# Layers 2 and 3 of a cross-attention chain: scores with the keys on the partitions, two tiles of queries at a time

## The reference

```python
qh = (q_in @ wq + bq).reshape(b, q_len, H, K)        # H = 16, K = 128
kh = (kv_in @ wk + bk).reshape(b, t, H, K)
vh = (kv_in @ wv + bv).reshape(b, t, H, K)
kh = jnp.concatenate([kh, broadcast(bias_k)], axis=1)  # one extra key and value
vh = jnp.concatenate([vh, broadcast(bias_v)], axis=1)
logits = jnp.einsum('bqhk,bthk->bhqt', qh, kh) / sqrt(K)
weights = jax.nn.softmax(logits, axis=-1)
ctx = jnp.einsum('bhqt,bthk->bqhk', weights, vh)
return ctx @ wo + bo
```

## Time and profile before

| | us |
|---|---|
| median of 3 runs | 1865.41 |
| profiled execution, its own time | 1866.31 |
| its span | 1864.4 |
| PE busy | 1711.7 |
| DVE busy | 1217.4 |
| ACT busy | 1018.2 |
| POOL busy | 393.0 |

### The profile page before, as it was taken

One profiled execution on the slowest core, in us unless ns is written; L12 is line 12 of the kernel. 1 busy time (PEld: TensorE's weight loads), 2 busy tenths in 40 slices (PEclk: granted clock), 3 DMA queues, 4 the chain that ended last, 5 costly groups with the idle time before them and its releaser, 6 DMA issues.

```text
span 1864.4 us, 31831 instructions
## 1 busy us (share of the span) xinstructions
PE 1711.7 (92%) x9942; PEld 1462.2 (78%) x9942; DVE 1217.4 (65%) x2487; ACT 1018.2 (55%) x1863; POOL 393.0 (21%) x320
## 2 busy tenths in 40 slices
PE   3698889897789999999999999799999999999997
PEld 2577777786568888888888877688888888888886
DVE  5577777777475666666665766766567566566664
ACT  2466666677344554554554556445455455555563
POOL 4456555542150000000000008410000000000063
PEclk8899999999789999999999999899999999999998
DMA  7767667766032101101101102420111011010021
GB/s 235 193 152 173 173 165 170 174 150 142 18 108 67 67 33 33 66 33 33 66 33 33 66 20 86 100 93 34 33 66 36 30 66 50 16 66 1 1 82 44
DMA packets 114097, 149.53 MB, mean 80 GB/s; under 512 B 25640, under 2 KB 99880, under 8 KB 114024
## 3 DMA queue, kind: packets, MB, share of 16 engines
q1 hardware_dynamic: 112680, 142.42, 27.8%
q10 hardware_dynamic: 1344, 6.19, 1.0%
HBM read 108.28 MB, written 3.42 MB: 60 GB/s over the span
## 4 chain that ended last, share of the span: by engine, by line
PE 71%; DVE 5%; ACT 2%; issue 2%; POOL 1%; DMA 0%; SPq 0%; DVEq 0%; ACTq 0%; POOLq 0%
PE ps L880 17%; PE ps L650 11%; PE ps L652 11%; PE ps L651 11%; PE ps L882 8%; PE ps L853 8%; PE ps L864 1%; DVE ar L1710 1%; DVE neg L1465 1%; ACT prob L1082 1%; PE ps L732 1%; DVE pt L1395 1%; PE ps L749 1%; DVE rr L1699 1%; DMA dk_raw<-in_bk 0%
## 5 line engine op out<-in xcount | busy, mean ns | idle before, releaser
L880 PE MATMUL ps<-cx,rr 128*128 128x512 f32 x1344 | 483.2, 402 | 2.2 <-issue 2.2
L1267 ACT ACTIVATE rr<-ps 128x512 fp32r<-128x512 f32 x336 | 200.5, 598 | 354.4 <-PE ps L853 352.7
L882 PE MATMUL ps<-cx,rr 128*128 128x256 f32 x1344 | 372.5, 277 | 0.0
L880 PEld LDWEIGHTS ps<-cx,rr 128*128 128x128 f32 x1344 | 252.2, 188 | 59.9 <-issue 6.8
L650 PE MATMUL ps<-ct,rr 128*128 128x500 f32 x672 | 279.7, 416 | 0.9 <-ACT ar L1238 0.6
L620 POOL TENSOR_SCALAR rr<-dvr,hsel 80x128 fp32r<-80x128 f32 x32 | 40.7, 1274 | 1093.1 <-DVE dvr L1605 993.4
L1586 DVE TENSOR_TENSOR rr<-ps,rr 128x512 fp32r<-128x512 f32 x336 | 231.7, 691 | 57.9 <-ACT rr L1267 41.3
L652 PE MATMUL ps<-ct,rr 128*128 128x500 f32 x672 | 261.1, 389 | 0.0
L651 PE MATMUL ps<-ct,rr 128*128 128x500 f32 x672 | 260.1, 387 | 0.0
L882 PEld LDWEIGHTS ps<-cx,rr 128*128 128x128 f32 x1344 | 253.2, 188 | 0.0
L1563 DVE TENSOR_REDUCE mx<-ps 128x1 f32<-128x500 f32 x336 | 227.5, 677 | 16.8 <-PE ps L652 9.5
(11 more groups left out here) (184 smaller groups left out, 3109.9 us busy)
## 6 DMA issues: line engine op xcount, KB each, us to landing
raw_t<-in_ctx_t SPq DMA_DIRECT2D x24, 1500.0 KB, 6.4
k<-khl SPq DMA_DIRECT2D x192, 187.5 KB
raw<-in_ctx SPq DMA_DIRECT2D x24, 1408.0 KB
raw<-stat_scratch ACTq DMA_DIRECT2D x7, 750.0 KB, 3.9
w_raw<-in_wq SPq DMA_DIRECT2D x32, 128.0 KB, 3.1
w_raw<-in_wk SPq DMA_DIRECT2D x32, 128.0 KB, 3.6
w_raw<-in_wv SPq DMA_DIRECT2D x32, 128.0 KB, 2.2
w_raw<-in_wo SPq DMA_DIRECT2D x32, 128.0 KB, 2.2
```

Source lines behind the costliest of these rows:

```text
L880: pe.matmul(ps[:, 6, :], pt[0:n, 0, c, :], cx[0:n, c, :], start=c == 0, stop=False, skip_group_check=True)
L882: mm = pe.matmul(ps[:, 6, 0:D], pt[0:n, 1, c, :], cx[0:n, c, 0:D], start=False, stop=c == CH - 1, skip_group_check=True)
L1267: act.activation(pt[:, 0, GRP * k:GRP * (k + 1), :], ps[:, 3 + k, :].rearrange("p (c q) -> p c q", q=P), ACT.Copy)\
```

## The change

The tiles of a batch are taken in four units: three pairs of tiles and one single tile. Keys are taken in 12 chunks of 125. The scores are computed with the keys on the partitions (weights: context chunk, moving: queries of the unit), two chunks to a PSUM bank, six banks. With that the probabilities need no transposes. The softmax needs the maximum over the keys, which now lie across partitions and banks: DVE keeps a running maximum over the banks, TensorE turns it, DVE reduces it along the row and joins the extra key's logit, TensorE spreads the negated maximum over the partitions, and DVE adds it to the scores. ACT takes exponentials and rounds them, in groups of 512 columns, and POOL makes the low halves. The sum over the keys comes from a column of ones beside the values. For the single tile high and low queries stand side by side; ACT copies the low part of the scores out and DVE adds it. The extra key's probabilities of a layer are sent in two parts (the first 53 tiles a step earlier). The output tile is scaled by ACT alone. Values are loaded by one DMA of 125 partitions. `low_scores`, `split_cx`, `split_ct` and `split_q` on ACT are copies of 256 (strided, from PSUM), 1024, 1000 and 512 columns.

Cut to its core (indices and semaphore arithmetic shortened where they do not matter; "..." inside a call stands for start and stop flags):

```diff
+KC = S // CH                      # 125 keys a chunk, CH = 12
+UNITS = (TILES + 1) // 2          # 4 units a batch: three pairs of tiles and one tile
+GROUPS = [CH // 2 if u < UNITS - 1 else CH // GRP for u in range(UNITS)]   # 6, 6, 6, 3
+W = 2 * P
+CW = 2 * D + 2
...
 def load_raw(r, b):
+    if r:
+        src = io["ctx"][bass.ds(b, 1), :, :].rearrange("o (c p) d -> p (o c) d", p=KC)
+        sp.dma_start(raw[0:KC, :, :], src).then_inc(s["raw_in"], 16)
+        return
...
 # POOL (new; DVE had these)
+def split_cx(i, b, k):            # k = 0, 1; the third third stays on DVE
+    wait_apart(pool, s["cx_hi"], 3 * bc + k + 1)
+    pool.tensor_tensor(cx[0:KC, v, D + 2:CW], raw[0:KC, v, :], f(cx[0:KC, v, 0:D]), ALU.subtract)
+def low_probs(i, b, u):
+    for k in range(GROUPS[u]):
+        wait_apart(pool, s["p_hi"], n + k + 1)
...
+        pool.tensor_tensor(group(p[:, 1, :, :], u, k), x, f(group(p[:, 0, :, :], u, k)), ALU.subtract)
+def attention(i):
...
+    if not pair(u):
+        wait_apart(pool, s["m_ready"], units(i, nb, nu) + 1)
+        for k in (0, 1):
+            split_cx(i, nb, k)
+    low_probs(i, nb, nu)
...
 # PE
+def scores(i, b, u, j):
+    for k in (0, 1):
+        v = slice(KC * (2 * j + k), KC * (2 * j + k + 1))
+        out = ps[0:KC, j, W * k:W * (k + 1)]
+        for e in range(DH):
+            if pair(u):
+                mm = three(pe, out, ct[:, 0, e, v], ct[:, 1, e, v], q[:, 0, e, :], q[:, 1, e, :], e == 0,
+                           e == DH - 1)
+            else:
+                pe.matmul(out, ct[:, 0, e, v], q[:, e, :, :].rearrange("p s r -> p (s r)"), ...)
+                mm = pe.matmul(out[:, 0:P], ct[:, 1, e, v], q[:, e, 0, :], ...)
+def all_scores(i, b, u, between):
+    for j in range(CH // 2):
+        pe.wait_ge(s["s_free"], CH // 2 * (n - 1) + j + 1)
...
+        scores(i, b, u, j)
+        if j == 1:
+            between()
+def turn_max(i, b, u, o_before):
+    pe.wait_ge(s["run_max"], units(i, b, u) + 1)
...
+    for k in range(4):
+        mm = pe.transpose(ps[:, 7, KC * to:KC * (to + 1)], run[0:KC, P * k:P * (k + 1)], ident[0:KC, 0:KC])
+def spread_max(i, b, u):
+    pe.wait_ge(s["neg_ready"], units(i, b, u) + 1)
+    for t in range(2 if pair(u) else 1):
+        mm = pe.transpose(ps[0:KC, 7, P * t:P * (t + 1)], negm[:, t:t + 1].to_broadcast([P, KC]), ident[:, :])
...
+def weighted(i, b, u, t, chunks):     # waits for p_hi and p_lo of each group
...
+        pe.matmul(ps[:, bank, 0:D + 2], hi, cx[0:KC, c, 0:D + 2], start=c == 0, ...)
+        pe.matmul(ps[:, bank, 0:D], hi, cx[0:KC, c, D + 2:CW], ...)
+        mm = pe.matmul(ps[:, bank, 0:D + 2], lo, cx[0:KC, c, 0:D + 2], ...)
...
 # PE, one step (unit b, u; nb, nu is the next unit)
+    all_scores(i, nb, nu, turn_before)
+    pe.wait_ge(s["o_back"], ...)
+    weighted(i, b, u, 0, range(0, 4))
+    turn_max(i, nb, nu, o_before())
+    weighted(i, b, u, 0, range(4, 9))
+    spread_max(i, nb, nu)
+    weighted(i, b, u, 0, range(9, CH))
+    if pair(u):
+        pe.wait_ge(s["m_ready"], units(i, nb, nu) + 1)
+        weighted(i, b, u, 1, range(0, 6))
+        turn_output(i, b, u, 0)
+        weighted(i, b, u, 1, range(6, CH))
...
 # ACT, one step
+    split_q(i, *later)
+    turn_output(i, *before, 1 if pair(before[1]) else 0)
+    if not pair(nu):
+        for j in range(CH // 2):
+            low_scores(i, nb, nu, j)          # PSUM to xp, 256 columns
+            if j % 2 and follows:
+                split_ct(*context, j // 2)
+    if not pair(u):
+        split_cx(i, nb, 0)
+        split_cx(i, nb, 1)
...
+    extra_prob(i, nb, nu)
+    exponentials(i, nb, nu, 0)
+    for k in range(GROUPS[nu]):
+        if k + 1 < GROUPS[nu]:
+            exponentials(i, nb, nu, k + 1)    # xp to xp, 512 columns
+        if k == 0 and not pair(u):
+            split_cx(i, nb, 2)
+        if k == 0:
+            scale_output(i, b, u, 0)
+        high_probs(i, nb, nu, k)              # xp to p_buf, 512 columns
+        if k == min(2, GROUPS[nu] - 1) and pair(u):
+            turn_output(i, b, u, 0)
+        if k == min(4, GROUPS[nu] - 1) and pair(u):
+            scale_output(i, b, u, 1)
...
 # DVE
+def running_max(i, b, u, order=range(CH // 2), between=()):
...
+        if pair(u):
+            if m == 0:
+                ins = dve.tensor_copy(run[0:KC, :], src)
+            else:
+                dve.wait_ge(s["run_step"], steps + m)
+                ins = dve.tensor_tensor(run[0:KC, :], src, run[0:KC, :], ALU.max)
+        else:
+            dve.wait_ge(s["b_out"], CH // 2 * ((i - 1) * B + b) + j + 1)
+            dve.tensor_tensor(x, high, x, ALU.add).then_inc(s["s_free"], 1)
...
+def row_max(i, b, u):
+    dve.tensor_reduce(mx2[:, 0:count], src, AX.X, ALU.max, negate=True).then_inc(s["red"], 1)
...
+    dve.tensor_tensor(negm[:, 0:count], mx2[:, 0:count], nlbq[:, bass.ds(g, count)], ALU.min)
+def shift(i, b, u, between=()):
+    dve.wait_ge(s["max_b"], n + 1)
+    dve.tensor_copy(m_b[0:KC, 0:P * count], ps[0:KC, 7, 0:P * count]).then_inc(s["m_ready"], 1)
...
+    for k in range(GROUPS[u]):
+        if pair(u):
+            dve.tensor_tensor(x, src, m, ALU.add).then_inc(s["s_free"], 1)
+        else:
+            dve.tensor_tensor(x, x, m, ALU.add).then_inc(s["shifted"], 1)
...
+def sums(i, b, u, t):
+    dve.tensor_tensor(total[:, :], ps[:, 6 + t, D:D + 1], extra[:, bass.ds(g, 1)], ALU.add)
+    dve.reciprocal(rinv[:, bass.ds(g, 1)], total[:, :]).then_inc(s["rinv_ready"], 1)
...
 # DVE, one step
+    sums(i, *before, 1)                       # if the unit before is a pair
+    if u == 0:
+        split_cx(i, b)
+    running_max(i, nb, nu, between=queries)   # the queries' low halves after the first bank
+    if follows:
+        split_ct(*context, 0)
+    row_max(i, nb, nu)
+    shift(i, nb, nu, (None, lambda: sums(i, b, u, 0)))
+    if follows:
+        split_ct(*context, 1)
+        split_ct(*context, 2)
...
 # SP: the extra key's probabilities, in two parts
+for first, end, k in ((0, GT - 3, 0), (GT - 3, GT, 1)):
+    sp.wait_ge(s["small_dve"], 7 * (i - 1) + 4 + 2 * k)
+    sp.dma_start(pb_d.rearrange("(g p) -> g p", p=P)[first:end, :], rows[0:end - first, :])
...
+    if k == 0:
+        for n in range(NS, 2 * NS - 1):
+            step_weights("o", i, n)
...
 # PE, queries(i) and attention(i): the first unit
+    first_scores(i, (0, 2))
     second_product("a", i, n)
+first_scores(i, (1, 3, 4, 5))
...
+turn_max(i, 0, 0, None)
+spread_max(i, 0, 0)
```

More of the change, by code:

```diff
@@ new lines, in extra_prob, with exponentials @@
+            def extra_prob(i, b, u):
+                wait_apart(act, s["neg_ready"], units(i, b, u) + 1)
+                for t in range(2 if pair(u) else 1):
+                    g = TILES * b + 2 * u + t
+                    ins = act.activation(extra[:, bass.ds(g, 1)], lbq[:, bass.ds(g, 1)], ACT.Exp, bias=negm[:, t:t + 1])
+                ins.then_inc(s["ex_done"], 1)
+            def exponentials(i, b, u, k):
+                if pair(u):
+                    wait_apart(act, s["s_free"], CH // 2 * units(i, b, u) + k + 1)
+                else:
+                    wait_apart(act, s["shifted"], 3 * ((i - 1) * B + b) + k + 1)
+                act.activation(group(xp, u, k), group(xp, u, k), ACT.Exp).then_inc(s["exp_done"], 1)
@@ new lines, in high_probs @@
+            def high_probs(i, b, u, k):
+                wait_apart(act, s["exp_done"], groups(i, b, u) + k + 1)
+                before = after(b, u, -1)
+                if zero(b) and u == 0:
+                    act.wait_ge(s["m2"], BASE["a", i] + H)
+                elif not pair(before[1]):
+                    wait_apart(act, s["pv"], tiles(i, b, u))
+                elif k < 5:
+                    wait_apart(act, s["pv_group"], parts(i, *before) + k + 1)
+                else:
+                    wait_apart(act, s["pv"], tiles(i, b, u))
+                act.activation(group(p_buf[u][:, 0, :, :], u, k), group(xp, u, k), ACT.Copy).then_inc(s["p_hi"], 1)
@@ new lines, in sums @@
+            def sums(i, b, u, t):
+                n, g = tiles(i, b, u) + t, TILES * b + 2 * u + t
+                dve.wait_ge(s["pv"], n + 1)
+                dve.wait_ge(s["ex_done"], units(i, b, u) + 1)
+                dve.tensor_tensor(total[:, :], ps[:, 6 + t, D:D + 1], extra[:, bass.ds(g, 1)], ALU.add)\
+                    .then_inc(s["sum_ready"], 1)
+                dve.wait_ge(s["sum_ready"], n + 1)
+                dve.reciprocal(rinv[:, bass.ds(g, 1)], total[:, :]).then_inc(s["rinv_ready"], 1)
@@ new lines, in attention, with step @@
+            def attention(i):
+                running_max(i, 0, 0, (0, 2, 1, 3, 4, 5))
+                row_max(i, 0, 0)
+                shift(i, 0, 0)
+                def step(b, u, last):
+                    end = last and not pair(u)
+                    (nb, nu), before = after(b, u), after(b, u, -1)
+                    later = after(b, u, 2)
+                    if not (zero(b) and u == 0) and pair(before[1]):
```

(22 more changed lines are left out.)

672 lines of the change are left out of this document (365 added, 307 removed).

## The result

The changed kernel takes 1944.93 us (median of 4 runs, 1938.15 to 1945.28) beside 1866.36 us of the kernel before in the same session (4 runs, 1865.3 to 1870.42): ratio 1.041, 95% interval 1.038 to 1.044. It is slower by 78.6 us; the forecast was 1870, in a range of 1822 to 1915. The profiled execution took 1938.15 us with a span of 1936.4, 72.0 more than the span before.

The account below looks back on a forecast made before the run. TensorE was taken as the bound. Per batch 65.0 us of work plus 3.8 of waits made 68.8 for 68.9; 1866.3 + 16 x (68.8 - 68.9) + 2 x 1.2 = 1867, raised for port turns to 1870, range 1822 to 1915.

Parts of the forecast that it names:

- TensorE's own work: Attention loops: scores, weighted sums and remaining transposes take 65.0 us a batch in place of 68.9.
- rival C: Weight loads bound TensorE's matmul stream: 0.13 us instead of 0.118 a matmul, 6 us a batch, 1940 us; chance 0.08.
- Waits before the unpaired tile: Step before the odd unit: TensorE waits 1.15 us for the output turn (ACT) and 0.9 for the maxima (DVE).
- After the unpaired tile, first shift: After the odd unit, with no second tile to run, TensorE waits 0.45 us for the first shifted bank.
- step 3: After the odd unit: 0.45 us for the first shift, 1.2 for maxima late by POOL's port, 2.5 if it wins twice.
- Step 2: Before the odd unit: ACT's and DVE's chains make TensorE wait 1.15 us for the output turn, 0.9 for the maxima.
- An edit costed at nothing: Values' load: one DMA in place of two costs nothing, since no one waits there.
- Rival B: DVE's two-input instructions lose port turns to POOL, 1.3 us each; two more a batch, +42 us, 1910; chance 0.22.
- Edges: Per layer, outside the steady batches: first unit +3.6 us, no port wait in first batch -1.2, extra key -1.2; net +1.2.
- The wait for the extra key's probabilities: Per layer: sent in two parts, the 2.12 us wait falls to about 0.9, a gain of 1.2, 0 at worst.

Follow-up runs that it names:

- e8: Changed kernel with e1's early query rounding, output turned after four banks behind four low-score copies, next queries' halves and context roundings moved later around the unpaired tile: 1861.96 us, ratio 0.9981.
- e4: Changed kernel with the odd unit's output turn after four banks of scores instead of two and context roundings behind the six low-score copies: 1965.62 us, ratio 1.0531.
- e5: e1 with the same two edits as e4 (later output turn, context roundings behind the low-score copies): 1885.12 us, ratio 1.0099.
- e1: Changed kernel with ACT rounding the third pair's queries at the end of the step before the batch's first, ahead of its exponentials: 1880.3 us, ratio 1.0074.
- e14: Changed kernel with 26 unused identity transposes put where TensorE waits 3.3 us for the maxima of each batch's second pair: 1929.0 us, ratio 1.0331.
- e13: Changed kernel with the 125-partition load of the values' context issued as two transfers, of 112 and 13 partitions: 1929.68 us, ratio 1.0341.
- e6: e1 with the last third of the values' low halves moved from DVE to POOL: 1893.88 us, ratio 1.0144.
- e0: The kernel before, unchanged, run again for a second trace: 1862.26 us (one run).
- e12: e8 with e13's split load, and in the last batch the first head's halves formed ahead of the next layer's context halves: 1850.48 us, ratio 0.9914.

## Why the prediction was wrong, step by step

- **TensorE's own work: nearly right.** 65.0 a batch forecast. In the changed kernel the 256-column matmuls start 0.12 apart, and a batch without its waits and its echo is 73.3 - 3.3 - 1.5 - 1.05 - 0.95 - 0.24 = 66.3 at the changed kernel, 67.5 - 1.3 = 66.2 in e8: 1.2 over the forecast. By the starts of TensorE's instructions in one batch of e8 (650.0 to 717.4 us) it is mostly the weighted sums, 31.6 us where 30.0 was forecast, and the pairs' scores, 26.0 for 25.5; the transposes take 3.2 for 4.0, the single tile's scores 5.5 for 5.4. Inside a row the 256 and 258 columns run at 0.118 to 0.12 as forecast; the first matmul behind another kind takes longer (0.20 us at 1360.05), and the forecast had no term for that. The pitch is not the 0.13 of rival C.
- **Waits before the unpaired tile: right.** 1.15 forecast for the turn and 0.9 measured, 0.9 for its maxima and 1.03 measured. In e4 and e5 the first went and the second grew by as much, so the two behave as one chain.
- **After the unpaired tile, first shift:** 0.45 forecast, 0.24 measured.
- **The failed step is 3, the maxima of the batch's first step: 1.2 us forecast (2.5 at the outside), 3.3 measured.** The step took DVE's queries' low half as waiting for POOL's port and free of ACT. By the text's own clock, with X the spreading of the maxima, ACT's last rounding of a unit stands at X + 8.6, and the queries' high half is queued behind it. The trace has X at 1344.02, the high half at X + 9.4, the low half at X + 10.2 to 12.1, the maxima until X + 15.6; the forecast had 8.95 for the low half's end and 13.1 for the maxima's. Against the forecast's 1.2, the low half ended 3.1 later, the five maxima took 0.6 less (0.72 apart, not 0.89), and TensorE came 0.4 later: 3.3. Step 2 counts that queue ("then queries, output, six copies"), step 3 left it out. e1 took exactly this wait away.
- **Missed altogether: the clock.** Waits were summed as if TensorE came back at full speed. Behind 12 of the 14 waits of 3.3 us it did not, and 1.5 us came on top each time, 18 us in all by the batches; e14 gave 14 to 16 of it back.
- **An edit costed at nothing: the single load for the values** ("no one waits there"). No one waits for the load, but a queue stands behind it: 12 to 15 us by the medians (e13), of which the two traces show 5.4, in a stage outside the two loops.
- **Rival B named the wrong resource.** Its time, 1910, is nearer than the forecast, but the port turned up only as lengths: DVE's L1775 took 1.82 us, as forecast for such instructions (1.9), and 0.68 at the shortest in these traces. Rival B needed DVE late by the port; it was late by ACT, and the port made it up to 1.1 us later. e6, which freed DVE of one such instruction, was slower.
- **Edges:** 1.2 us a layer forecast, 5.0 and 7.6 measured (below; the second with all that follows layer 3's loop). The wait for the extra key's probabilities fell from 2.1 to 1.1 us, near the forecast 0.9. Not forecast were 2.5 us for the output's turn at the end of each loop (L988, until 1130.48 and 1830.27 us), each with the low clock behind it; the rest was not taken apart.

The sum, in the two profiled executions: the seven batches between the turns ahead of the second pair take 28.7 us more in layer 2 and 28.0 in layer 3 (1287.82 to 1798.07), the edges of layer 2 have 5.0 (33.7 - 28.7), what else follows its end 7.6 (35.6 - 28.0), and layer 1 ended 2.7 later: 72.0. The 2.7 is small for what the load costs because the kernel before ended layer 1 late there (551.1, and 546.9 in e0). The work saved does pay once the queues are in order. By e8's batches it is 16 x (68.9 - 66.2) = 43 us, of which waits take 14 x 1.3 = 18; e12 is faster by 15.5 (1866.01 - 1850.48), which leaves some 9 for edges.

## What to carry to other kernels

When work moves from one engine to a chain of three, write the in-order queue of every engine into the schedule for each kind of step, the odd one and the one after it too. The waits here came from small preparing instructions (a 0.6 us rounding of queries for two steps later) behind a long row of softmax work; moved a step forward they cost nothing and won 62 to 65 us. Put such a preparation where its engine last has nothing urgent, and count a wait of TensorE of some 3 us at nearly half again its length: the low clock followed 12 of 14 of them here, at 1.5 us each. When a tile's partition count changes from 128, look at each transfer's DMA share and at what is queued behind it.

## What the runs showed of the hardware that was not expected

- After 3.3 us without a matmul the granted clock went to 0.50 for about 3 us in 12 of 14 cases of the changed kernel and stayed at 1.00 in the other two. At 1359.64 us it was still 1.00 for the first microsecond of matmuls; at 1098.22 it was 0.50 from the first one on. Waits of 0.9 to 1.1 us had no such effect. Those of 2.1 to 2.2 us had it each time in e4 (as at 702.50 us, 2.18) and four times of fourteen in e5 (not at 768.08, 2.13); what sets these apart stays open.
- A transfer to 125 partitions moved 118 GB/s at a DMA share of 0.37, split into 112 and 13 the same stretch had 210 GB/s at 0.91.
- A matmul of 128 columns behind one of 256 (the unpaired tile's scores, each with its own weight load) costs 0.06 us and the pair 0.23: 0.06 was the lower of the forecast's bounds, 0.108 was taken. The timeline of TensorE in the changed kernel:

```profile
688.02 0.33 PE L947 MATMUL ps<-rr,ct 128*125 128x256 f32 x1
688.19 0.22 PE L949 MATMUL ps<-rr,ct 128*125 128x128 f32 x1
688.25 0.33 PE L947 MATMUL ps<-rr,ct 128*125 128x256 f32 x1
```

From 688.02 to 688.19 the wide one has 0.17, from there to 688.25 the narrow one 0.06.
